# Moving two weight-splitting rounds behind a layer norm, exponentials between evictions, and the output store into the last layer

## The reference

```python
x = x + attention(x, ctx; L0) @ Wo + bo             # front layer 0
q, k, v = x @ Wq + bq, ctx @ Wk + bk, ctx @ Wv + bv # front layer 1
w = softmax(q @ k.T / 16, axis=1)                   # over the tokens, not over the context
x = w @ v + x
x = (x - mean(x)) * rsqrt(var(x) + 1e-6) * gamma + beta
x = x + attention(x, ctx; L2) @ Wo + bo             # front layer 2
for layer in range(6):                              # 16 heads of 64
    tn = ln(t, norm_g, norm_b); t = mha(tn, tn, self_mask) @ sa_ow + sa_ob + t
    tn = ln(t, norm_g, norm_b); t = mha(ctx, tn, ctx_mask) @ ca_ow + ca_ob + t
    tn = ln(t, pre_g, pre_b);   t = t + relu(tn @ w1 + b1) @ w2 + b2
```

## Time and profile before

| | us |
|---|---|
| runs | 2820.63, 2822.99, 2823.05 |
| profiled execution, its own time | 2825.08 |
| its span | 2823.3 |
| busy: PE, PEld | 2736.2, 2300.6 |
| busy: DVE, ACT, POOL | 1690.4, 1278.1, 1169.2 |
| mean granted TensorE clock | 0.987 of full |
| the front (from the start to the first transposes of Start) | 0 to 172.8 |
| Start | 172.8 to 218.8 |
| main loop, 24 iterations | 218.8 to 2817.9 |
| the store | 2817.9 to the end |

### The profile page before, as it was taken

How to read it: one execution, slowest core, us unless ns; L and a number is a source line. 1 busy time by engine, 2 the same in 40 slices (tenths; PEclk the granted TensorE clock), 3 DMA queues, 4 the chain that set the end, 5 groups by cost and what they waited for, 6 DMA issues and landing times.

```text
span 2823.3 us, 64336 instructions
## 1 busy us (share of the span) xinstructions
PE 2736.2 (97%) x24290; PEld 2300.6 (81%) x24290; DVE 1690.4 (60%) x6337; ACT 1278.1 (45%) x4195; POOL 1169.2 (41%) x1452
## 2 busy tenths in 40 slices
PE   8689999999999999999999999999999999999988
PEld 7668888888888888888888888888888888888876
DVE  2356576576566565665665665765765665656654
ACT  3244454454454444444544544544544544444442
POOL 2314445344444344354444454444444443433432
PEclk9899999999999999999999999999999999999999
DMA  6333434426335236244336334335343344332320
GB/s 199 120 111 135 154 92 142 120 89 200 104 121 164 76 123 193 77 145 154 90 109 207 93 136 147 98 116 163 118 154 105 113 137 119 108 103 76 104 75 14
DMA packets 178777, 346.00 MB, mean 123 GB/s; under 512 B 18269, under 2 KB 142758, under 8 KB 169382
## 3 DMA queue, kind: packets, MB, share of 16 engines
q1 hardware_dynamic: 168390, 195.08, 24.1%
q0 software_dynamic: 10080, 146.81, 14.3%
HBM read 303.18 MB, written 38.67 MB: 121 GB/s over the span
## 4 chain that ended last, share of the span: by engine, by line
PE 82%; POOL 6%; DVE 4%; issue 2%; DMA 2%; SPq 1%; ACT 1%; DVEq 0%; POOLq 0%; ACTq 0%
PE proj L713 19%; PE sum L1075 16%; PE score L713 14%; PE proj L733 8%; PE sum L713 6%; PE sum L733 5%; PE score L924 3%; PE proj L1096 3%; PE sum L948 3%; PE proj L1033 2%; POOL rstd L610 2%; POOL stage_parts L578 2%; PE tr L1033 1%; PE tr L935 1%; PE tr L1075 1%
## 5 line engine op out<-in xcount | busy, mean ns | idle before, releaser
L663 POOL TENSOR_TENSOR prob<-prob,rtotal 128x375 f32<-128x375 f32 x672 | 543.5, 811 | 584.2 <-DVE rtotal L1722 583.0
L1155 ACT ACTIVATE prob<-prob,negmax 128x375 f32<-128x375 f32 (+1 forms) x686 | 418.1, 609 | 389.5 <-DVE negmax L1713 370.3
L1075 PE MATMUL sum<-pT,ctx 32*128 32x224 f32 (+1 forms) x4608 | 500.4, 358 | 1.1 <-DVE qcT L1703 1.1
L1075 PE MATMUL tr<-pT,ctx 32*128 32x224 f32 (+1 forms) x4608 | 500.3, 358 | 0.0
L1075 PEld LDWEIGHTS sum<-pT,ctx 32*128 32x128 f32 (+1 forms) x4608 | 417.1, 185 | 53.6 <-issue 46.2
L1713 DVE CUSTOM_DVE_ANT_0 prob<-score,cbias 128x375 f32<-128x375 f32 x672 | 357.9, 533 | 135.7 <-PE score L713 131.4
L1075 PEld LDWEIGHTS tr<-pT,ctx 32*128 32x128 f32 (+1 forms) x4608 | 417.1, 185 | 0.0
L1731 DVE STREAM_TRANSPOSE pT<-prob 128x384 f32<-128x384 f32 x672 | 373.4, 559 | 0.7 <-issue 0.7
L713 PE MATMUL score<-ctx_parts,qc_high 128*128 128x376 f32 x1344 | 369.5, 356 | 3.4 <-DVE negmax L1713 3.4
L617 POOL TENSOR_TENSOR prob<-prob,rtotal 112x448 f32<-112x448 f32 x192 | 178.6, 930 | 408.8 <-DVE rtotal L1579 408.8
L1247 ACT ACTIVATE prob<-prob,negmax 112x112 f32<-112x112 f32 x768 | 287.6, 380 | 81.7 <-DVE negmax L1597 81.7
(11 more groups left out here) (305 smaller groups left out, 5184.6 us busy)
## 6 DMA issues: line engine op xcount, KB each, us to landing
w_vq_parts<-sa_v_parts POOLq DMA_DIRECT2D x24, 2048.0 KB, 8.2
w_kf<-ff_w SPq DMA_DIRECT2D x48, 1024.0 KB, 7.0
w_kf_parts<-sa_k_parts POOLq DMA_DIRECT2D x23, 2048.0 KB, 8.4
w_vq_parts<-sa_q_parts POOLq DMA_DIRECT2D x23, 2048.0 KB, 9.2
ctx<-ctx SPq DMA_DIRECT2D x192, 176.0 KB
stage<-sa_kv SPq DMA_DIRECT2D x24, 512.0 KB, 3.9
sa_v_parts<-stage_parts SPq DMA_DIRECT2D x12, 1024.0 KB, 5.1
sa_q_parts<-stage_parts SPq DMA_DIRECT2D x12, 1024.0 KB, 4.7
```

Source lines behind the costliest of these rows:

```text
L663: pool.tensor_tensor(row, row, rtotal[:, G * SG + i:G * SG + i + 1].broadcast_to([P, S2]), ALU.mult).then_inc(prob_ready, 1)
L1075: ins = pe.matmul(bank[:, 0:HT * R], ctx4[keys_of, m // (HALVES // NB), j, :], pT[keys_of, m % 2, :, j * R:(j + 1) * R], start=j == 0, sto ...
L1155: act.activation(o, i, ACT.Exp, bias=negmax[0:rows, col:col + 1], scale=scale, accum_out=total[0:rows, col:col + 1]).then_inc(exp_ready, 1)
```

## The change

Three edits. In the front, POOL does four of the six rounds of weight parts, then the four `inverse_std`, and then the last two rounds. In Start, ACT does the exponentials of the first two groups in pairs of heads, each pair behind one eviction of the second half of the queries and keys; PE makes the scores of groups 4 and 5 between the two batches' values; ACT's and DVE's later steps are put in another order. In the last layer, SP stores each finished pair at the start of the next iteration, ahead of the mask load, and the last pair batch by batch.

```diff
+    ROUNDS_BEFORE_NORM = LAYER_ROUNDS - 2
@@ SP
+            def store_pair(p, batches=range(NB)):
+                first, n = p * NB + batches[0], len(batches)
+                sp.dma_start(out[first:first + n].rearrange("b s e -> s b e"), t_all[:, first:first + n, :]).then_inc(stored, 16)
@@ SP, head of each iteration
+                if l == L - 1 and p > 0:
+                    for name in ("sum1", "proj1"):
+                        sp.wait_ge(taken[name], at.emptied(name, 0))
+                    store_pair(p - 1)
                 if it < LAST:
                     sp.wait_ge(smask_used, it + 1)
                     load_pair_smask(next_p)
@@ SP, end
-            sp.wait_ge(taken["proj1"], Place(MAIN_LOOP, LAST).emptied("proj1", FF_OUT + 1 - V2 - HC))
-            sp.dma_start(out.rearrange("b s e -> s b e"), t_all[:, :, :]).then_inc(stored, 16)
-            sp.wait_ge(stored, 16)
+            end = Place(MAIN_LOOP, LAST)
+            sp.wait_ge(taken["sum1"], end.emptied("sum1", BEFORE_SUMS["sum1"] + HALVES + 2))
+            store_pair(PAIRS - 1, (0,))
+            sp.wait_ge(taken["proj1"], end.emptied("proj1", FF_OUT + 1 - V2 - HC))
+            store_pair(PAIRS - 1, (1,))
+            sp.wait_ge(stored, 16 * (PAIRS + 1))
@@ POOL, front
-            for r in range(LAYER_ROUNDS):
+            for r in range(ROUNDS_BEFORE_NORM):
                 parts_of_weights(r)
             for u in range(NU):
                 inverse_std(at, 1, u)
+            for r in range(ROUNDS_BEFORE_NORM, LAYER_ROUNDS):
+                parts_of_weights(r)
@@ PE, Start
-            values(at, range(NB * V2), (tnT_next,), (w_vq[:, 0, :, :],))
+            values(at, range(V2), (tnT_next,), (w_vq[:, 0, :, :],))
+            self_scores(at, 2)
+            values(at, range(V2, NB * V2), (tnT_next,), (w_vq[:, 0, :, :],))
             self_transposes(at, 0)
             self_transposes(at, 1)
-            self_scores(at, 2)
             self_sums(at, 0)
@@ ACT, Start
-            for half in (0, G):
-                for c in range(half, half + G, 2):
-                    queries(at, c)
-                for c in range(half, half + G, 2):
-                    keys(at, c)
-            self_exponentials(at, 0)
+            for c in range(0, G, 2):
+                queries(at, c)
+            for c in range(0, G, 2):
+                keys(at, c)
+            for g, evicted in enumerate((queries, keys)):
+                for c in range(0, G, 2):
+                    evicted(at, G + c)
+                    self_exponentials(at, g, range(c, c + 2))
             values(at, 0)
-            self_exponentials(at, 1)
+            self_exponentials(at, 2)
             values(at, 1)
-            self_exponentials(at, 2)
             self_exponentials(at, 3)
             self_probabilities(at, 0)
             self_exponentials(at, 4)
+            self_probabilities(at, 2)
+            self_exponentials(at, 5)
             attended(at, 0)
-            self_exponentials(at, 5)
-            self_probabilities(at, 2)
             self_exponentials(at, 6)
             self_exponentials(at, 7)
@@ DVE, Start
             values(at, 0)
             self_reciprocals(at, 1)
+            self_maxima(at, 4)
+            self_maxima(at, 5)
             values(at, 1)
             self_reciprocals(at, 2)
+            self_probabilities(at, 1)
             self_reciprocals(at, 3)
-            self_probabilities(at, 1)
-            self_maxima(at, 4)
-            self_maxima(at, 5)
-            self_reciprocals(at, 4)
             self_probabilities(at, 3)
-            self_reciprocals(at, 5)
             self_maxima(at, 6)
             self_maxima(at, 7)
+            self_reciprocals(at, 4)
+            self_reciprocals(at, 5)
             attended(at, 1)
```

## The result

The changed kernel takes 2807.37 us, the median of four runs (2804.24 to 2809.44); the kernel before took 2822.51 (four runs, 2820.63 to 2823.05). The ratio is 0.9947, 95% interval 0.9935 to 0.9959: 15.1 us less. The forecast was 2807.7.

What follows compares the result with a forecast made beforehand. PE, busy for 97% of the span, bounds the main loop; gains lie where it idles, chiefly the front's norm, held by POOL's queue order. 11.4 + 1.0 + 2.9 = 15.3 us off 2822.99 gives 2807.7, range 2803.5 to 2813.

Steps and rivals of the forecast that it cites:

- Term 1, the norm: Front: with the powers ahead of POOL's last two rounds, PE's last layer 2 transposes start 13.0 us earlier.
- term 1: The front's whole gain: 13.0 from the norm less 1.6 at the multiplications, 11.4 us.
- Term 1, the multiplications: Layer 2: DVE's eight multiplications of probabilities, partly held by POOL's later gamma and bias work, lose 1.6 us.
- POOL holds DVE more than I count: Rival, layer 2's multiplications: 5.0 us lost in place of 1.6, giving 2811.1 us; chance 0.12.
- Term 1, the clock: Front: PE's granted clock falls again in its idle time, about 113 to 118 us; gain 0.
- the clock stays at 2.4 GHz: Rival, front: PE keeps its full clock through the norm, winning 2.5 us more, 2805.2 us; chance 0.12.
- Term 2, Start: Start: a shorter later ACT queue brings ACT's norm 1.3 us and the last head sums 1.0 us earlier.
- the eight exponentials leave the queue: Start: eight exponentials (3.0 us) fit between ACT's evictions and leave its later queue; 3.0 was the gain's upper bound.
- Term 3, the store: Kernel's end: a last store of 112 KB lands in 2.1 us in place of 5.0, winning 2.9 us.
- The rival of the late masks: Last layer: stores delay the mask loads by 6.0 us, three times, 18.0 lost, giving 2825.7 us; chance 0.02.
- the powers aren't what the norm waits for: Rival, front: something behind the powers is just as late, leaving only terms 2 and 3, 2819.1 us; chance 0.02.

Runs made afterwards that it cites:

- e5_wait: The whole change, plus POOL waiting for DVE's fourth normalisation before its fifth round of weight parts; 2805.77 us, ratio 0.9946.
- e8_split: The kernel before, plus one POOL wait for DVE's split of the tokens ahead of the first iteration's residual add; 2818.78 us, ratio 0.9989.
- e1_front: The kernel before with only the front's edit (four rounds, the powers, two rounds); 2811.05 us, ratio 0.9962.
- e9_late: As e4_order, plus POOL's sixth round waiting for DVE's last multiplication of layer 2; 2800.80 us, ratio 0.9924 to the kernel before.
- e12_both: e9_late plus the one POOL wait of e8_split in Start; 2799.08 us, ratio 0.9921 to the kernel before.
- e0_whole: The whole change again with no further edit, timed beside its parts; 2806.89 us, ratio 0.9947 to the kernel before.
- e6_nostart: The whole change with PE, ACT and DVE of Start in the order of before, so front and store edits alone; 2807.22 us, ratio 0.9948.
- e7_busy: The whole change, with PE making the third pair's transposes in layer 2 nine times over to stay busy; 2805.44 us, ratio 0.9944.
- e2_start: The kernel before with only the Start edits of PE, ACT and DVE; 2820.10 us, ratio 0.9997.
- e4_order: The whole change, plus POOL's wait for the fourth normalisation before its fifth round and the gamma and bias work ahead of its sixth; 2803.26 us, ratio 0.9936.
- e11_exps: The kernel before with only the first two groups' exponentials placed between ACT's evictions in Start; 2822.54 us, ratio 1.0002.
- e3_store: The kernel before with only the stores in the last layer changed; 2818.62 us, ratio 0.9989.

## Why the prediction was right, step by step

**Term 1, the norm (13.0 predicted).** From the full bank to the transposes 19.76 became 6.68: 13.1. The powers were done at 107.86 (said: by 109), the normalisation was 3.52 long (3.5), the transposes at 111.47 (said: 112.6; everything came 1.1 earlier from the start of the program on). That POOL's cast and subtraction would set the normalisation's end was the decision that mattered in it: 15.9 without, and e5_wait shows that it is POOL.

One point in it was probably wrong in size. I took the whole 13.0 off the median. But the end of that wait before is set by a chain of five stores and loads, and the profiled execution of before had a late one. The cast of its second round (first row) against e8_split's:

```profile
66.13 1.04 POOL L576 CAST stage_parts<-stage 128x1024 fp32r<-128x1024 f32 x1 [8.16 <-DMA stage<-sa_kv]
```

```profile
63.27 1.04 POOL L576 CAST stage_parts<-stage 128x1024 fp32r<-128x1024 f32 x1 [8.15 <-DMA stage<-sa_kv]
```

In the four profiles of other kernels without the front's edit the transposes came at 122.0 to 123.6, not 125.60; with the edit and without e5_wait's wait, where PE's own work sets them, at 111.5 to 113.0. The usual gain there is thus 9 to 12, about 11. e1_front measures 10.2 for term 1, where the sum had 11.4; its interval of 7 to 14 us allows both. I took 13.0 in full off a median that lies 2.1 us under this execution, as if those 2.1 lay anywhere else in the program. But in the other traces the transposes come at 123.6 at the latest, so at least 2 us of the lateness lie in the chain that the change takes off the path.

**Term 1, the multiplications (-1.6 predicted).** 0.68, 1.12 and 1.53 for the first three, five at 0.41: 0.3, 0.7 and 1.1 held, where I had placed 0.3, 0.7 and 0.9, and 2.1 in their sum. From transposes to the last one's end it was 24.92 before and 26.02 after, 1.1 lost. The rival "POOL holds DVE more than I count" fell: with 5.0 lost it would have been 29.9. Its mechanism stands, however, and it is what e9_late wins back. The Trainium skill's rule ("SBUF — State Buffer", "Who interferes with whom"), an exclusive lock for an instruction's length, fits these rows: each of the four held instructions of after (the normalisation and three multiplications) ends 0.15 to 0.22 us behind one of POOL's. The rows of Start's split fit it the other way round, with POOL's instructions the longer ones.

**Term 1, the clock (0 predicted).** It fell, as said, though at 109 to 116 and not at 113 to 118, so the rival "the clock stays at 2.4 GHz" fell. What I had not seen is the second stretch. Before, the granted clock was at 0.53 from 151 to 158; after, at 0.53 from 136 to 147, longer by 3 or 4 us. From the last multiplication to Start it took 22.3 us before and 23.2 after, 0.9 more. With the 1.1 above that is 2.0 in all, against the 1.6 of the sum. That POOL's hold brings the longer low stretch isn't shown: e9_late, whose eight multiplications run free, has it too (0.50 over 129:139, 23.3 us), while e12_both, the same program up to there, has the short one (0.51 over 135:141, 22.3 us).

**Between Start and values** the profile shows 1.7 us won that no step of mine has. It is one stretch of matmuls at a lower or at the full clock. e9_late and e12_both are one program up to there, and their first sixteen matmuls for the queries read:

```profile
154.90 3.27 PE L729 MATMUL proj<-tnT_next,w_vq 128*128 128x224 f32 x16 [1.21 <-ACT tnT_next L1246]
```

```profile
157.27 4.95 PE L731 MATMUL proj<-tnT_next,w_vq 128*128 128x224 f32 x16 [1.21 <-ACT tnT_next L1248]
```

The granted clock around the first was 1.00, and from 158 to 161 us, within the second, 0.50. So the order of instructions alone doesn't decide it. Yet Start to values is 17.4 us in all five traces with the change's order of the front (after, e0_whole, e1_front, e6_nostart, e7_busy), and 19.1 in all five without any change of the front; of the four with a wait in it, one has 17.4 and three 19.1. Six traces have the long second stretch of the clock and then 17.4 us from Start to values (those five and e9_late); e5_wait has the long one and 19.1 us; the other seven have the short one and 19.1. So the 0.9 lost and the 1.7 won mostly go together, 0.8 won on balance. Whether the change brings them, and by what, stays open.

**Term 2, Start (1.0 predicted).** In the profile ACT's norm came 17.47 us behind the values in place of 18.23: 0.8, where I said 1.3. The second value eviction lost 1.16 (1.0 said), and from there to the norm it was 1.9 shorter (2.3 said). The last head sums came 2.4 us nearer (2.7 in e0_whole); 1.8 of that is Start's edit (e2_start). The rest goes with the granted clock, which over the 6 us ahead of those sums was 0.76 in after and 0.82 in e0_whole, and 0.52 to 0.54 in the four kernels that win 1.8 with Start's edit (e2_start, e5_wait, e4_order, e12_both). The reading "the eight exponentials leave the queue" failed as a reason for the eight alone (e11_exps). The split, which I had as held by POOL as before and priced at nothing, was the larger part: the wait alone wins 1.7 (e8_split), and Start's order with a held split only 0.5 (e9_late). The medians don't confirm the size: 1.1 from e2_start, whose interval contains nothing, and nothing between e6_nostart and the whole. Another 1.5 us was won between the last head sums and the last addition, which the sum doesn't have. It goes with the clock again: over the first 8 us behind the last head sums the granted clock was 0.62 before and 0.76 after, which at a busy PE is about 1.1 us by estimate (8 times 0.14). The other traces go the same way: those with 0.61 to 0.65 (e3_store, e11_exps, e9_late) take 2600.4 to 2600.9 us from there to the last addition, the seven with 0.70 to 0.74 take 2599.5 to 2600.1. Only e1_front (1.00) and e6_nostart (0.79), with 2599.7 both, aren't shorter still; their low stretches begin at other places. What sets the length of that stretch stays open.

**Term 3, the store (2.9 predicted).** The last store landed in 1.9 us (2.1 predicted), the span ends 3.1 us sooner behind the last addition, and e3_store measures 2.6. By the line in the Trainium skill, "DMA: Bandwidth & Descriptors", section "Anatomy of one DMA — SWDGE (gpsimd) path", it would be an estimate of 2.3 us; the page fits that line to DMAs issued by GpSimd, and these are SP's. The masks lost nothing: SP's two issues took 0.33 and 0.46, and the rows of `sbias` lie 13.6 us behind `attended` in both kernels. The rival of the late masks fell. Its price was too high as well: only two of the three stores have a mask load behind them, since the last iteration loads none, so it was two times 6.0 and not three.

**The rival "the powers aren't what the norm waits for"** (2819.1) fell with e1_front.

So the sum, 15.3, met 15.1. The mechanism of term 1, which is most of it, is shown, and so is the store's. That the two numbers agree to 0.2 us is luck: term 1 was probably about 1 too large, what term 2 holds in the medians is known no better than to 1 or 2 us, and the profiles have gains and losses of the clock behind the norm (0.9 lost, 1.7, 0.6 and about 1.1 won) that the sum put at 0.

## What to carry to other kernels

Where an engine is waited for, look at what stands ahead in its queue and isn't wanted yet; here two rounds of POOL's work cost about 10 us. Then look at what it will run beside in its new place: POOL's elementwise work in SBUF holds DVE's, and placing it with two waits (e9_late) took the gain from 14.3 to 20.7 us. A wait holds where an order only happens to: Start's order gave a free split in some kernels and a held one in e9_late. And when an execution is slower than its median, ask in which stage, before a gain is counted from it.

## What the runs showed of the hardware

- A pair of DVE instructions of 112x256 took 0.74 alone and 3.52 beside POOL's cast and subtraction of 128x1024; DVE's split of 128x448 took 1.53 with POOL kept back by a wait and 5.34 beside POOL's residual add and casts. Eight multiplications of 0.41 sum to 3.3 alone and to 5.1 to 6.8 beside POOL. It goes the other way too: beside a split of 1.57 POOL's product took 1.62 in place of 0.93, and its residual add 1.66 in place of 1.28.
- TensorE's granted clock was 0.50 in one execution and 1.00 in another at the same instructions in the same order (e12_both and e9_late), which cost 1.7 us.
- Start-up varies: POOL had the second round's data at 62.9 to 66.3 us in different executions. Through the chain of stores and loads that lateness reaches the first point where PE waits for its end.
- Keeping PE busy with repeated transposes went with a granted clock of 1.00 over 106 to 118 us, and 1.9 us were won there. e9_late and e4_order had 1.00 over the same time without them.
